# Key rows of an edge group laid over the partitions by TensorE instead of by a DMA from DRAM

## What is computed

```python
h = relu(layernorm(x)); x = x + L0(h)      # 3 rounds of  segment_sum(x[row] * norm, col), norm from degrees
h = relu(layernorm(x)); x = x + L1(h)      # segment_sum(h[src] * weight, dst) / max(deg, 1), two linear maps
h = relu(layernorm(x)); x = x + L2(h)      # Chebyshev gates: two propagations with -dis[src] * weight * dis[dst]
h = relu(layernorm(x)); x = x + L3(h)      # attention over the edges (src, dst), 4 heads of 16
```

## Time and profile before

| | us |
|---|---|
| median of 3 runs | 2480.02 (2478.61 to 2483.64) |
| the profiled execution | 2481.01 |
| its span, first to last instruction | 2479.3 |
| DVE busy | 1763.7 (71%) |
| POOL busy | 1562.3 (63%) |
| PE busy | 1168.0 (47%) |

### The profile page before, as it was taken

One profiled execution on the slowest core, in us unless ns is written; L12 is line 12 of the kernel. 1 busy time (PEld: TensorE's weight loads), 2 busy tenths in 40 slices (PEclk: granted clock), 3 DMA queues, 4 the chain that ended last, 5 costly groups with the idle time before them and its releaser, 6 DMA issues. The chain is left out here.

```text
span 2479.3 us, 40227 instructions
## 1 busy us (share of the span) xinstructions
PE 1168.0 (47%) x12261; PEld 597.3 (24%) x12261; DVE 1763.7 (71%) x3795; ACT 646.2 (26%) x1920; POOL 1562.3 (63%) x1191
## 2 busy tenths in 40 slices
PE   1111111111111111111110461699989998999998
PEld 1111111111111111111110120233434443333334
DVE  9999999999999999999981100102321257999996
ACT  0000000013233133131120112200000136888884
POOL 1688788888888888888888777000000036788884
PEclk6555555555555555555555685799999998999997
DMA  7677777667767777766656797999999775333332
GB/s 245 208 220 219 201 208 233 164 152 214 229 202 213 243 202 208 244 196 174 176 128 173 238 364 207 376 369 357 370 397 345 283 237 160 103 106 106 106 106 52
DMA packets 268041, 541.20 MB, mean 218 GB/s; under 512 B 132065, under 2 KB 140702, under 8 KB 258238
## 3 DMA queue, kind: packets, MB, share of 16 engines
q1 hardware_dynamic: 127485, 288.88, 33.4%
q10 hardware_dynamic: 26000, 245.78, 25.3%
q0 software_dynamic: 114480, 5.67, 11.4%
HBM read 371.92 MB, written 168.31 MB: 218 GB/s over the span
## 5 line engine op out<-in xcount | busy, mean ns | idle before, releaser
L1159 POOL DMA_INDIRECT table<-held x782 | 1215.6, 1554 | 333.5 <-issue 308.3
L685 DVE SCALAR_TENSOR_TENSOR resident<-resident,ring,banks 128x1280 bf16<-128x1280 f32 (+9 forms) x790 | 692.1, 942 | 0.3 <-DVE ring L671 0.3
L994 PE MATMUL banks<-ring,resident 128*128 128x6 bf16 x4345 | 128.6, 167 | 1022.9 <-DVE held L694 1022.9
L1108 PE MATMUL banks<-ring,scaled 128*64 128x512 f32 x1250 | 314.2, 614 | 165.8 <-DVE scaled L793 81.2
L1369 DVE TENSOR_TENSOR att<-att,banks_d 128x1024 f32<-128x1024 f32 (+1 forms) x350 | 366.0, 1085 | 36.0 <-POOL att L1434 28.7
L1434 POOL TENSOR_SCALAR att<-att 128x1024 f32<-128x1024 f32 (+1 forms) x350 | 320.3, 934 | 85.4 <-ACT att L1337 85.4
L994 PEld LDWEIGHTS banks<-ring,resident 128*128 128x128 bf16 x4345 | 122.0, 104 | 1034.3 <-DVE held L694 1034.3
L460 ACT ACTIVATE held<-held 128x128 f32<-128x128 f32 x575 | 171.8, 301 | 762.4 <-DMA weights_dram<-held 753.1
L1337 ACT ACTIVATE att<-banks_d 128x1024 f32<-128x1024 f32 (+1 forms) x350 | 302.3, 915 | 79.4 <-PE banks_d L1457 79.4
L1207 POOL DMA_DIRECT2D parts_dram<-scaled x7 | 5.4, 778 | 448.5 <-DVE scaled L865 448.3
L677 DVE SCALAR_TENSOR_TENSOR scaled<-resident,ring,banks 128x1280 bf16<-128x1280 f32 x156 | 235.2, 1545 | 21.1 <-issue 18.1
(11 more groups left out here) (220 smaller groups left out, 1323.7 us busy)
## 6 DMA issues: line engine op xcount, KB each, us to landing
table<-acc ACTq DMA_DIRECT2D x100, 800.0 KB
held<-table ACTq DMA_DIRECT2D x24, 3200.0 KB
ring<-counts_dram SPq DMA_DIRECT2D x60, 1280.0 KB, 13.6
ring<-weights_dram SPq DMA_DIRECT2D x60, 1280.0 KB, 11.8
resident<-keys_dram SPq DMA_DIRECT2D x79, 640.0 KB
weights_dram<-held ACTq DMA_DIRECT2D x25, 1600.0 KB
counts_dram<-c_tile ACTq DMA_DIRECT2D x24, 1600.0 KB, 5.4
count<-counts_dram SPq DMA_DIRECT2D x150, 256.0 KB, 2.7
```

What stands on the lines that cost most here:

```text
L685: ins = nc.vector.scalar_tensor_tensor(equal[b][:, OWN_AT[j]:OWN_AT[j + 1]], key_row[:, b, j * P:GE], keys[:, bass.ds(g * G + j, 1)], own_ ...
L994: nc.tensor.matmul(sums, equal[b][:, at:at + P], parts_g[:, b, j, :], start=False, stop=True, skip_group_check=True)
L1108: ins = nc.tensor.matmul(sums, xs[:, prop % 2, s], rows, start=s < 2, stop=True, skip_group_check=True)
L1159: nc.gpsimd.indirect_dma_start(out=table, out_offset=bass.IndirectOffsetOnAxis(ap=cell[:, slot, j:j + 1], axis=0), in_=amount[:, slot, j, ...
```

## The change

- `keys_dram`, its two stores and all 79 loads of rows go. SP has nothing to issue between the small inputs of the setup and the counts.
- The row of a group is made by PE: `make_row` transposes ten columns of keys, each broadcast over 128 columns, into PSUM. There are two rows in PSUM, of three banks each. DVE puts the ten columns into `keys_now` at the end of the `compare_own` of the group two before.
- The masks move from PSUM to SBUF. `totals` moves to the two last banks.
- The degrees of a group are added by PE into the group's own `totals` bank, and DVE adds them to `deg_in` in `choose_cells`, in place of one copy at the end.
- `compare_own` gets a wait for the next group's row, since row numbers for L692 share a bank with the second row.

The core of the diff:

```diff
-    key_row = take([P, 2, GE], F32)
+    masks = take([P, P + GE], F32)
+    centred_words = take([P, T * D], F32)
...
+    keys_now = take([P, 2, G], F32)
...
-    masks = banks[:, 0:3].rearrange("p a c -> p (a c)")
-    totals, turned, degrees = banks[:, 3:5], banks[:, 5:7], banks[:, 7]
+    key_row = [banks[:, 3 * b:3 * b + 3].rearrange("p a c -> p (a c)")[:, 0:GE] for b in range(2)]
+    numbers = banks[:, 5, GE - 2 * BANK:]
+    totals, turned = banks[:, 6:8], banks[:, 3:5]
...
-            def load_row(g, b):
-                sp.dma_start(key_row[:, b, :], keys_dram[bass.ds(g, 1), :].to_broadcast([P, GE])
-                             ).then_inc(row_landed[b], 16)
...
+            nc.vector.memset(k["deg_in"][:], 0.0)
...
+            nc.vector.tensor_copy(keys_now[:].rearrange("p b j -> p (b j)"), keys[:, 0:2 * G]).then_inc(first_keys, 1)
...
-                        equal_tail[:, b, i, :], key_row[:, b, :], keys[:, bass.ds(g * G - TAIL + i, 1)], all_mask,
+                        equal_tail[:, b, i, :], key_row[b], keys[:, bass.ds(g * G - TAIL + i, 1)], all_mask,
...
+                if more:
+                    ins = nc.vector.tensor_copy(keys_now[:, b], keys[:, bass.ds((g + 2) * G, G)])
                 ins.then_inc(compared, 1)
+                dve.wait_ge(row_ready, g + 2 if more else NG)
...
+                nc.vector.tensor_tensor(k["deg_in"][:], k["deg_in"][:], totals[:, b, in_degrees], ALU.add
+                                        ).then_inc(degrees_added, 1)
...
-                    ins = nc.tensor.matmul(degrees[:, 0:T], is_row[:, b, j, :], is_tile[:, b, j, :], start=False,
+                    ins = nc.tensor.matmul(totals[:, b, in_degrees], is_row[:, b, j, :], is_tile[:, b, j, :], start=False,
...
+            def make_row(g, b):
+
+                for j in range(G):
+                    ins = nc.tensor.transpose(key_row[b][:, j * P:(j + 1) * P],
+                                              keys_now[:, b, j:j + 1].to_broadcast([P, P]), k["ident"][:])
+                ins.then_inc(row_ready, 1)
+
+            pe.wait_ge(first_keys, 1)
+            make_row(0, 0)
+            pe.wait_ge(needs_ready, 4)
+            pe.wait_ge(masks_set, 4)
+            make_row(1, 1)
+            pe.wait_ge(equal_ready, 1)
+            make_row(2, 0)
             add_up(0, 0, carry=False)
...
+            def next_add_up(g, b):
+                pe.wait_ge(equal_ready, g + 1)
+                make_row(g + 2, b)
+                add_up(g, b)
```

More of the change, by code:

```diff
@@ L260, in tables_and_products @@
     needs_ready, group_started, group_taken = sem("needs_ready"), sem("group_started"), sem("group_taken")
-    row_landed = [sem(f"row_landed{b}") for b in range(2)]
+    row_ready, first_keys = sem("row_ready"), sem("first_keys")
     masks_set, compared, tail_compared = sem("masks_set"), sem("compared"), sem("tail_compared")
-    equal_ready = sem("equal_ready")
+    equal_ready, degrees_added = sem("equal_ready"), sem("degrees_added")
     totals_ready, totals_free = sem("totals_ready"), sem("totals_free")
@@ L366, in _ @@
                 sp.dma_start(to, frm.rearrange("(a f) -> a f", a=1)).then_inc(small_landed, 16)
[L368 to L375, removed]
             def tiles_stored(last_tile):
@@ L734, in _ @@
             dve.sem_inc(slots_free, SLOTS)
[L735 removed]
+            dve.wait_ge(row_ready, 1)
             compare_own(0, 0)
[L737 removed]
+            dve.wait_ge(row_ready, 2)
             compare_tail(1, 1)
@@ L740, in _, with next_group, next_pair @@
             compare_own(1, 1)
-            def next_group(g, b, n, slot):
-                dve.wait_ge(row_landed[b], 16 * n + 16)
+            def next_group(g, b, slot, more=True):
+                dve.wait_ge(row_ready, g + 1)
                 compare_tail(g, b)
-                compare_own(g, b)
+                compare_own(g, b, more)
                 choose_cells(g - 1, 1 - b, slot)
-            def next_pair(i, slots):
-                next_group(2 * i + 1, 1, i, slots[0])
-                next_group(2 * i + 2, 0, i + 1, slots[1])
-            dve.wait_ge(row_landed[0], 32)
+            def next_pair(i, slots, more=True):
+                next_group(2 * i + 1, 1, slots[0], more)
+                next_group(2 * i + 2, 0, slots[1], more)
+            dve.wait_ge(row_ready, 3)
             compare_tail(2, 0)
@@ L761, in _ @@
             for i in range(SLOTS // 2 * ROUNDS + 1, NG // 2):
-                next_pair(i, [(2 * i + n - 1) % SLOTS for n in range(2)])
+                next_pair(i, [(2 * i + n - 1) % SLOTS for n in range(2)], more=i < NG // 2 - 1)
             choose_cells(NG - 1, 0, (NG - 2) % SLOTS, final=True)
-            link(nc.vector.tensor_copy(k["deg_in"][:], degrees[:, 0:T]))
+            dve.wait_ge(degrees_added, NG)
             dve.sem_inc(scratch_read, 1)
@@ L980, in _ @@
             pe.wait_ge(small_cleared, 3)
-            nc.tensor.matmul(degrees[:, 0:T], zero_bf[:], zero_bf[:, 0:T], start=True, stop=False, skip_group_check=True)
             pe.wait_ge(edges_read, 4)
@@ L986, in add_up @@
                 pe.wait_ge(totals_free, g + 1)
-                nc.tensor.matmul(totals[:, b, 0:8 * G], zero_bf[:], zero_bf[:, 0:8 * G], start=True, stop=False,
+                nc.tensor.matmul(totals[:, b, 0:in_degrees.stop], zero_bf[:], zero_bf[:, 0:in_degrees.stop], start=True, stop=False,
                                  skip_group_check=True)
```

35 lines of the change are left out of this document (13 added, 22 removed).

## The result

| | before | after |
|---|---|---|
| median of the runs beside each other, us | 2483.64 (2478.61 to 2487.02) | 2470.66 (2467.79 to 2472.14) |
| the profiled execution | 2481.01 | 2467.79 |
| its span | 2479.3 | 2466.0 |

The ratio of after to before is 0.9949, with a 95% interval of 0.9938 to 0.9959: faster by some 13 us. The prediction said 2470.0, in a range of 2464 to 2484, and faster as the likeliest sign. That 2470.66 lies so near to 2470.0 is in part luck: the prediction took 10 us off 2480.02, and beside the changed kernel the kernel before had a median of 2483.64.

What follows compares the result with a forecast made beforehand. The prediction took POOL's issue of scatters to bound the groups. From the profiled 2481.0 us it took 12 for DMA traffic and added 2 at the start: 2471.0, so a median of 2470, range 2464 to 2484.

Steps and rivals of the forecast that it cites:

- What bounds the groups: In the group loop, POOL's issue of scatters sets the pace at 18.6 us a group; DVE needs 16.0 us.
- The DMA traffic: Between 120 and 1322 us, POOL's waits from row loads meeting bursts go: 12 us less, with 0 and 16 as ends.
- row-by-row count of eight gaps: POOL's eight long gaps after row loads, 175.18 to 1041.85 us, capped at 1.9 us each: 11.7, with smaller ones 13.7 us.
- the bystanders: At POOL's long gaps, bursts alone cause the waits and row loads do not; only the start counts: 2482 us, chance 0.25.
- The start: Up to POOL's scatter at 75.30 us, added work and a wait delay DVE and POOL by 2 us, from 1.5 to 2.5.
- the wait for the totals: At the start, PE's row of group 2 delays group 0's sums, so DVE waits 0.5 to 1.3 us.
- The steady groups: In the loop, DVE rises to 16.3 us a group, still 2.3 below POOL's 18.6; PE's added rows cost nothing.
- rival 3: In the loop, comparisons slowed by reading the row from PSUM make DVE the bound: 2528 us; chance 0.05 together with rival 4.
- the wait for slots: DVE's wait for POOL to free slots, 28.2 us before, covers some 23 us of added work and stays above zero.
- rival 4: In each group, rows come late and DVE waits for PE; over 2.3 us a group would matter; chance 0.05 with rival 3.
- Rival 2: In the loop, 77 added copies of ten keys each hold a scatter, 13 us: 2495, or 2483 with the gain; chance 0.06.
- The sum: For the whole kernel: profiled execution 2481.0 - 12 + 2 = 2471.0, so a median of 2470 us.

Runs made afterwards that it cites:

- cells_early: Changed kernel with DVE choosing a group's cells before the next group's ten own comparisons, and PE doing sums before the row: 2459.14 us, ratio 0.9914.
- rows_half: rows_back with each unused row load cut to 640 of its 1,280 keys, as many loads: 2474.09 us, ratio 0.9965.
- rows_moved: rows_back with each load released by POOL's landed groups instead of DVE's comparisons, and only 67 rows loaded: 2477.76 us, ratio 0.998.
- rows_back: Changed kernel with the key stores and all 79 row loads put back at their old pace, into an unread place: 2484.66 us, ratio 1.0007.
- sums_first: Changed kernel with PE adding up group 0 before it makes the row of group 2: 2469.02 us, ratio 0.9945.
- copies: Changed kernel with four more f32 copies of 128x128 within SBUF on DVE in each group: 2477.19 us, ratio 0.9983.
- copies_psum: Changed kernel with four more f32 copies of 128x128 a group on DVE, read from PSUM: 2479.29 us, ratio 0.9988.

## Why the prediction held, step by step

**What bounds the groups: right.** `cells_early` gave DVE 58 us of waiting, and the end still came 11.5 us earlier; PE got 170 us of work in the change itself. In the row experiments the time rises with POOL's lag. From the 31st to the 671st scatter POOL falls behind the changed kernel by 5.7, 7.4 and 19.5 us in `rows_half`, `rows_moved` and `rows_back`; their profiled executions took 8.1, 10.0 and 19.5 us longer, and their medians are 3.4, 7.1 and 14.0 us higher.

**The DMA traffic, -12 us: right in kind, and larger.** From the 31st to the 671st scatter it is -15.0 us, inside the bounds of 0 and 16. Putting the loads back cost 14.0 us in the median and 19.5 us of lag in its trace, so the cause is shown, and the size to some 5 us. The row-by-row count of eight gaps had given 13.7. It was short for two reasons. The cap of 1.9 us a collision is not a bound: the gap before 175.18 is 2.4 us longer than the fixed one and is gone in the changed kernel, as are all the others. And the wait of 1.1 us (before 422.86) without a row load shortly before it, which stood for the bystanders, went too (0.5 and 0.8 us). Of the 1.7 us taken off for bursts that meet other scatters nothing was needed here. The wait of 4.08 us before 101.35 stayed, as said (4.13), and so did the one before the 31st scatter (1.04 us before, 1.38 after).

**The start, +2 us: right in kind, too small.** It is 2.3 us at the first scatter and 2.6 behind the gap, a tenth beyond the upper bound of 2.5. The step that was mis-sized is the wait for the totals. DVE's timeline, and PE's beside it, the answers to the earlier trace rows:

```profile
48.78 0.18 DVE L691 TENSOR_TENSOR deg_in<-deg_in,banks 128x25 f32<-128x25 f32 x1 [1.67 <-PE banks L984]
```

```profile
44.23 2.40 PE L998 MATMUL banks<-ident,held 128*128 128x128 f32 x10 [12.57 <-DVE held L680]
...
46.76 1.63 PE L981 MATMUL banks<-ring,resident 128*128 128x6 bf16 x55
```

Ten transposes take 2.40 us, not 1.4 to 2.2. With that, the slack of 0.9 us leaves 1.5 us, where the sum had 0.5 to 1.3 and took 0.9; the trace has 1.67. Of the two rows of transposes in the earlier trace rows, the longer series (21 in 4.71 us) was the nearer, and still 7% short. The copies and additions are near what was said: L672 and L691 take 0.16 and 0.18 us, and overlap with their neighbours. `sums_first` takes this wait away and gets 1.5 us back at the gap. Two landing waits behind the gap then add 0.4 us, which makes the 3.0 at the 31st scatter.

**The steady groups: right in size, one statement wrong.** DVE, one group of the steady loop, the answer to the earlier trace rows:

```profile
614.32 1.55 DVE L660 SCALAR_TENSOR_TENSOR scaled<-banks,ring,resident 128x1280 bf16<-128x1280 f32 x1
...
625.98 0.17 DVE L672 COPY held<-ring 128x10 f32 x1
...
627.95 0.17 DVE L691 TENSOR_TENSOR deg_in<-deg_in,banks 128x25 f32<-128x25 f32 x1
...
630.46 1.55 DVE L660 SCALAR_TENSOR_TENSOR scaled<-banks,ring,resident 128x1280 bf16<-128x1280 f32 x1 [0.20 <-issue]
```

The period is 16.1 us where 16.3 was said: both new instructions run half under their neighbours. A comparison with its row in PSUM and its mask in SBUF takes 1.55 us as with them the other way round, so rival 3 falls. The wrong statement is that the wait for slots would still be above zero. It is zero. The 28.2 us of the earlier trace rows were cover for some 23 us of predicted work, and the cover should have been set against POOL too: POOL runs up to 12.0 us earlier and frees its slots earlier, so DVE meets no full slots. `rows_back` bears this out: with the same work on DVE and POOL late again, the wait for slots is back, 19.0 us. Nothing came of it, since the layer norm behind DVE waits 52.8 us as before.

One line of the changed kernel invites a false reading. DVE's waits, from 33 to 1400 us (total, times, longest):

```profile
DVE scaled L660 <- PE banks L998: 14.7, 27, 0.7
```

It looks as if the comparisons waited for PE's rows (rival 4). But the same instruction waits as long, every second group, in the kernel before, where its line is

```profile
DVE scaled L677 <- issue: 18.1, 35, 0.7
```

In the changed kernel another 3.6 us in 9 waits of this instruction are put down to issue, which makes 18.3 us in 36, against 18.1 in 35. It is the turn of the loop, 0.5 us every two groups. The row of the group after next happens to be finished at 630.48 when L660 starts at 630.46, and the wait is put down to it. Rival 4 falls.

**Rival 2, the copy that holds POOL: not seen.** Scatters take 1553 ns in the mean with one copy of ten keys a group and 1552 with four of 128x128 besides. The rule of the Trainium skill in SBUF, State Buffer (section "SBUF: two separate sides"), that an f32 copy within SBUF on DVE locks GpSimd out of the port, would have made `copies` slower than `copies_psum`. An estimate by that rule: 77 groups with 0.62 us of such copies could hold POOL up to 48 us. The measurement decides: `copies` took 2477.19 us and `copies_psum` 2479.29, and over the 47 groups from the 201st to the 671st scatter, with 29 us of such copies, POOL in `copies` falls 0.1 us behind the changed kernel.

**The sum: right, in part by luck.** +2.6 up to the gap, +0.4 up to the 31st scatter, -15.0 up to the 671st and +2.0 behind it give -10.0, and the last scatter starts at 1541.99, where the prediction has it near 1542. But the terms were not 12 and 2. The gain at the waits was 3.0 us larger, the loss at the start 1.0 us larger, and the 2.0 us that went in the streaming of the counts have no term of their own in the sum. That they cancel is luck. The load of the last tile moved by -10.6. The median came out 13 us lower; the interval of the ratio, 10 to 15 us, holds both figures, and the rest lies behind the load, see above.

## What to carry to other kernels

- When the bounding engine issues small DMAs and waits for their landing, a large transfer can be on its path, whoever needs it: 0.64 MB beside a burst of 3.2 MB held it for up to 2.4 us in the kernel before. Set its long gaps beside the list of what was issued 5 to 15 us earlier; taking out a transfer that an idle PE could replace was worth about the sum of those gaps here.
- Look first at the gaps at the start. Here the bounding engine did not get a late start back, and changing the order on an engine with slack (DVE) to feed it sooner brought 11.5 us, nearly as much as the change itself.
- Before moving a burst, ask which other burst waits for the same signal or for the same queue: it may only be pushed onto the next victim.

## What the runs showed of the hardware

- **The granted clock of PE did not matter in the groups.** It differs between executions of one kernel: those of the changed kernel with a mean clock of 0.965 and 0.966 over the program took 2471.11 and 2469.24 us, those with 0.69 took 2467.79, 2470.66 and 2472.14. Of the profiled executions, those of `rows_back`, `rows_half` and `rows_moved` had 1.00 (2.4 GHz) through the groups, all others 0.50 (1.2 GHz). Stretches of `rows_back` and then of `cells_early` (length, busy PE, PEld, DVE, ACT, POOL (instructions), clock, DMA share, GB/s):

```profile
600.00:660.00 60.00, 16.12 (x318) 14.33 (x317) 58.42 (x147) 21.18 (x102) 49.94 (x34) 1.00 0.69 200
```

```profile
600.00:660.00 60.00, 14.84 (x289) 13.27 (x289) 56.44 (x146) 10.66 (x51) 50.05 (x33) 0.50 0.69 211
```

  Ten f32 transposes take 2.40 us at 1.00 in `rows_back` and 2.39 us at 0.50 in the changed kernel, and the 55 small products of the sums take 1.63 us in both. What decides between the two levels was not looked into. It is not the row loads alone: 5 of the 11 executions of `rows_back` had a mean of 0.69, and 2 of the 5 of the changed kernel had 0.97.
- **More instructions in a loop can stall its engine at each outer turn.** With the four copies DVE stands still for 3.4 to 6.4 us once in 205 us, which is 12 of its groups or one turn of its outer loop, waiting for nothing that the profile shows. The changed kernel has no such stall. DVE's waits in `copies`, one such place, and the queue of instruction loads, which had 44 packets and 0.36 MB in the changed kernel:

```profile
DVE scaled L661 <- issue: 26.0, 14, 6.4
```

```profile
287.37 1.55 DVE L661 SCALAR_TENSOR_TENSOR scaled<-banks,ring,resident 128x1280 bf16<-128x1280 f32 x1 [6.40 <-issue]
```

```profile
q14 instruction: 70, 0.57, 0.1%
```

  That the stalls are loads of code is the reading nearest to these numbers. It was only argued, since no run changed the length of the code alone. `copies_psum` has them too (26.3 us in 13 waits). The stalls and the copies put the last cell numbers of DVE (L709 in the changed kernel, L712 here) off from 1310.7 us to 1376.5 in `copies` and 1390.4 in `copies_psum`, and the layer norm's wait falls from 52.8 to 0.3 us.
